# First attention scores interleaved with half tiles of the last second MLP product, in a fused decoder kernel

## The chip, the cores and the metric

One core of a Trainium2 chip runs the whole kernel as one program. Five engines work beside each other, each through its own list of instructions in order, and wait for each other on semaphores: TensorE (PE, matrix products), VectorE (DVE), ScalarE (ACT), GpSimd (POOL) and SyncE (SP), which here only issues DMA transfers. The metric is the device time of one execution in microseconds (us), as the median of several runs. Smaller is better.

## The reference

Four sequences (B = 4) of T = 512 tokens with D = 256 features go through three parts, each followed by a layer norm:

```
x = layernorm(x + recurrent_block(x))      # gated recurrence, then an MLP:
                                           #   x1 + silu(ln(x1) @ w_mlp1.T + b1) @ w_mlp2.T + b2
x = layernorm(x + attention(x, ctx, ctx))  # 16 heads of 16 features, causal softmax
x = layernorm(x + experts(x))              # 48 experts, each takes its top 64 tokens
```

The change lies at the border of the first and the second part: the second MLP product of the last sequence, and the attention scores of the first one.

## The kernel before

**First stage.** Sequences go through the recurrent block one after the other. `expand` makes the 1024 hidden features in eight products, ACT applies silu (`hidden`), and `shrink` makes the second MLP product: for each of TT = 4 token tiles of 128, eight fp32 products of 128x256 summed in PSUM banks 6 and 7 (line 1706). When the whole of it is done PE raises `m2`, DVE adds it to the residual in `X` (`ln_out`, line 1046) and `ln_out_norm` takes statistics (lines 920, 924), waits for 1/sqrt of the variance from POOL (`root`, lines 715 and 717) and normalizes (line 933). For the last sequence, parts of the attention's preparation for sequence 0 are already mixed with `expand`: transposes of its tokens and the key, query and value projections (`early`, `middle`, `late`). Projected keys and queries are split in bf16 pieces, written to DRAM (`key_out`, `query_out`; lines 557 and 561) and read back by head group (`keys_in`, `queries_in`, line 572: six transfers each) into `KTs` and `QTs`. These share SBUF with the MLP weights: the part of groups 0 and 1 may be filled when the first MLP product is done (`m1`), that of groups 2 and 3 only when `m2` is raised.

**Attention.** 16 heads are 4 groups of 4. Each group is four slots j (key tiles of 128). For each group there are 11 PSUM bank fillings of raw scores, over three banks (`scores`: a causal mask product at line 1819, then the scores at line 1823). DVE takes their maxima (`maxima`, line 1133), `negate` splits the negated maxima in bf16 pieces, PE transposes them (`minus_max`, line 1833) and ACT copies them under the queries (line 1506). Then PE makes the scores again, now less the maximum (`shifted`, line 1849), ACT takes the exponential (line 1518), POOL sets what lies above the diagonal to zero (line 797) and PE multiplies with the values (`values`, line 1862). In the slots of one group, the raw scores of the next group are mixed with the shifted ones of this one, so the first group's raw scores stand alone, ahead of all slots. POOL also fills ones rows of `KTs` for each group (line 775, semaphore `ones`) and adds a bias row to the tokens of a sequence (line 790). `TASKS` puts the projections of the next sequence in the slots: (0, 0) holds the transposes of sequence 1 (`query_in`, line 1761), (0, 3) its query projection (line 1782).

The order on each engine is that of the code. PE before runs the whole last `shrink`, waits for `ln3` (DVE has added the product to the residual), makes the eleven fillings for group (0, 0), fills time with five products that nobody reads (`run_idle`, line 1635), then `minus_max` and the slots. POOL waits with the ones rows of groups 2 and 3 for `m2` and then with `root` for the statistics, all ahead of its first slot. SP issues `query_out(0)` behind `keys_in(0, 0)`, which waits for `m1`.

Of the kernel before, what the change touches and what calls it, by code (L numbers as in the profile page):

```python
# [11 lines left out]
ACT = mybir.ActivationFunctionType  # L12
AX = mybir.AxisListType

P = 128
B, T, D = 4, 512, 256
TT = T // P
# [6 lines left out]
MT = MLP // P  # L24
NH, HD = 16, 16
GH = 4
NG = NH // GH
# [104 lines left out]
def build(nc, x, ctx_in, w_in, w_gate, w_out, coupling, w_mlp1, w_mlp2, w_q, w_kv, w_o, w_r,  # L132
# [7 lines left out]
    with stack:  # L140
        def sb(name, shape, dt=F32):
            return stack.enter_context(nc.sbuf_tensor(name, shape, dt))
# [39 lines left out]
        rden = sb("rden", [P, TT, GH])  # L182

# [314 lines left out]
        def _(sp):  # L498
# [98 lines left out]
            tokens_in(1)  # L597
            sp.wait_ge(b2_out, 16 * NPC)
            sp.wait_ge(m1.s, m1.now(B - 1, MT))
            keys_in(0, 0)  # L600
            query_out(0)
# [78 lines left out]
        def _(pool):  # L680
# [91 lines left out]
            for g in range(NG):  # L772
                if g == 2:
                    pool.wait_ge(m2.s, m2.now(B - 1, 1))
                pool.tensor_copy(KTs[SK:SX, GH * g:GH * g + GH, :],
                                 own[SK:SX, :].unsqueeze(2).to_broadcast([SX - SK, GH, T]))\
                    .then_inc(ones, 1)
            pool.wait_ge(ones, NG)
            root(ln3, rs3, B - 1, 1 + 2 * TT)
            pool.wait_ge(rs3.s, rs3.now(B - 1, 2))  # L780
# [12 lines left out]
            def pool_slot(b, g, j, prev, then, *steps):  # L793

                pool.wait_ge(exq.s, exq.now(b, g * NSH + FIRST[j] + len(SHARED[j])))
                pool.sem_inc(pool_held, 1)
                pool.affine_select(out=pb[j % 2][:, :, 0:P], in_=pb[j % 2][:, :, 0:P],  # L797
                                   compare_op=ALU.is_ge, fill=0.0, base=0,
                                   pattern=[[0, GH], [1, P]], channel_multiplier=-1)\
                    .then_inc(msk.s, 1)  # L800
                for name, c, k in steps[0] + steps[1] + steps[2] + steps[3]:
                    if name == "bias":
                        with_bias(c)
                    elif name == "stats":
                        root(ln4, rs4, c, 2 + 2 * TT)
# [99 lines left out]
        def _(dve):  # L905
# [143 lines left out]
            def ln_out_norm(b):  # L1049

                dve.wait_ge(ln3.s, ln3.now(b, 1))
                statistics(ln3, X, b * TT, b, 1)
                norm(ln3, rs3, X, lambda t: X[:, b * TT + t, :], b * TT, b)
# [21 lines left out]
            with dve.Fori(0, B - 2) as b:  # L1075
                recurrence(b + 1)
                ln_out(b)
                ln_out_norm(b)
            recurrence(B - 1, then=False)
            ln_out(B - 2)  # L1080
            ln_out_norm(B - 2)
# [112 lines left out]
            def dve_slot(b, g, j, prev, then, *steps):  # L1194
# [12 lines left out]
                if j == 2 and then is not None:  # L1207
                    negate(*then)
                dve_do(steps[3])
# [3 lines left out]
            ln_out(B - 1)  # L1213
# [5 lines left out]
            ln_out_norm(B - 1)  # L1219
# [185 lines left out]
        def _(act):  # L1405
# [154 lines left out]
            act_do(late)  # L1560
            spare_banks[:] = 5, 7
# [66 lines left out]
        def _(pe):  # L1628
# [61 lines left out]
            def expand(b, tiles):  # L1690

                pe.wait_ge(xe2.s, xe2.now(b, KT))
                for m in tiles:
# [5 lines left out]
                    mm.then_inc(m1.s, 1)  # L1699

# [136 lines left out]
            def shifted(b, g, j):  # L1837

                w = T - j * P
                for n, heads in enumerate(SHARED[j], FIRST[j]):  # L1840
                    if j == 0 and heads[0] % 2 == 0:
                        pe.wait_ge(nte.s, nte.now(b, 2 * g + heads[0] // 2 + 1))
# [108 lines left out]
            shrink(B - 1, range(TT))  # L1951
            for k in range(2):
                pe.wait_ge(*read_by[k])

            pe.wait_ge(silu.s, silu.now(B - 1, MT))
            pe.wait_ge(ln3.s, ln3.now(B - 1, 1))
            read_by.update({0: None, 1: None})
            spare_banks[:] = 5, 7
            for share in SCORED:
                for banks in share:  # L1960
                    scores((0, 0), banks)
            run_idle(5, 4)
            minus_max(0, 0)
            pe.wait_ge(ones, NG)
# [209 lines left out]
```

## Time and profile before

| | |
|---|---|
| time, median of 3 runs | 659.65 us (658.91 to 660.65) |
| time of the profiled execution | 660.65 us |
| its span, first to last instruction | 658.9 us |
| mean granted TensorE clock | 0.964 of full |
| last second MLP product on PE | 166.1 to 180.1 us |
| first shifted scores of group (0, 0) on PE | 191.00 us |
| first shifted scores of group (0, 1) on PE | 206.77 us |

Positions are microseconds from the span's start. The profiled execution's own time is 1.75 us above its span and 1.0 us above the median. In rows of the trace, "x8" after an operation is a count of merged instructions, and what stands in brackets is the idle time of the engine ahead of them and who ended it. One fp32 product is often shown as two instructions.

### The profile page before, as it was taken

What the parts mean: (1) busy time and instruction counts of PE and PEld (TensorE: products, weight loads), DVE (VectorE), ACT (ScalarE), POOL (GpSimd) and SP (SyncE); (2) the same over time, 40 slices, a digit from 0 to 9 for tenths busy, and PEclk for the clock granted to TensorE, in tenths of its full rate; (3) what the DMA queues carried; (4) which work ended last, traced back from release to release, by engine and by line L of the source; (5) the groups of instructions that cost most, each with busy time, mean ns of one, the idle gap of its engine ahead of it and who ended that gap; (6) DMA issues with size and microseconds to landing.
All of it is one profiled execution on the core that took longest, in us unless ns stands there. A gap on an engine that the chain in (4) does not pass through costs nothing.

```text
span 658.9 us, 11028 instructions
## 1 busy us (share of the span) xinstructions
PE 577.2 (88%) x3856; PEld 333.5 (51%) x3856; DVE 380.2 (58%) x792; ACT 275.8 (42%) x460; POOL 186.3 (28%) x231
## 2 busy tenths in 40 slices
PE   6899999999979889989999988850499999999994
PEld 3648586655834535555464444320144554545581
DVE  5874737333176767685697767069633433434645
ACT  4260512425046656666667657500043333333204
POOL 3133232061123123121222222110234444342233
PEclk9999999999989899999999989985699999999998
DMA  8696000013530641155025731049179999999873
GB/s 264 212 381 239 0 0 0 1 67 98 163 94 0 186 119 49 49 178 176 17 91 166 228 157 65 0 154 422 35 270 386 395 395 397 402 392 391 273 268 128
DMA packets 43583, 120.38 MB, mean 183 GB/s; under 512 B 6212, under 2 KB 28308, under 8 KB 40468
## 3 DMA queue, kind: packets, MB, share of 16 engines
q1 hardware_dynamic: 38372, 113.20, 47.5%
q0 software_dynamic: 4320, 6.03, 4.2%
q10 hardware_dynamic: 848, 0.60, 0.3%
q8 instruction: 24, 0.39, 0.2%
q14 instruction: 19, 0.16, 0.1%
HBM read 95.88 MB, written 21.83 MB: 179 GB/s over the span
## 4 chain that ended last, share of the span: by engine, by line
PE 72%; DVE 11%; ACT 7%; DMA 4%; issue 3%; SPq 1%; POOL 1%; ACTq 0%; DVEq 0%; POOLq 0%
PE PS L2026 13%; PE PS L1697 8%; PE PS L1706 8%; PE PS L1782 4%; PE PS L1862 4%; PE PS L1849 4%; PE PS L1823 4%; PE PS L2058 4%; PE PS L2039 4%; DVE Mx L1133 2%; ACT arena L1506 2%; PE PS L1801 2%; PE PS L1666 2%; PE PS L1819 2%; PE PS L1774 2%
## 5 line engine op out<-in xcount | busy, mean ns | idle before, releaser
L1133 DVE TENSOR_REDUCE Mx<-PS 128x1 f32<-128x384 f32 (+3 forms) x176 | 103.6, 634 | 40.0 <-PE PS L1823 38.7
L1518 ACT ACTIVATE arena<-PS 128x512 f32<-128x512 f32 (+1 forms) x176 | 90.3, 559 | 48.1 <-PE PS L1849 46.7
L797 POOL TENSOR_SCALAR_AFFINE_SELECT arena<-arena 128x512 f32<-128x512 f32 x64 | 40.9, 638 | 165.0 <-ACT arena L1518 165.0
L1849 PE MATMUL PS<-arena 108*128 108x512 bf16 (+3 forms) x256 | 62.3, 306 | 11.7 <-ACT arena L1506 5.7
L1823 PE MATMUL PS<-arena 96*128 96x128 bf16 (+3 forms) x256 | 62.8, 303 | 0.0
L1697 PE MATMUL PS<-arena 128*128 128x512 f32 x128 | 56.1, 593 | 3.2 <-ACT arena L1423 1.6
L1706 PE MATMUL PS<-arena 128*128 128x256 f32 x256 | 55.9, 379 | 0.0
L1635 PE MATMUL PS<-ident,identb 128*128 128x512 bf16 x82 | 23.7, 434 | 33.2 <-DVE Y L1258 29.3
L1300 DVE COPY X<-PS 128x512 f32<-128x512 f32 x24 | 16.6, 691 | 61.6 <-PE PS L2026 61.6
L1706 PEld LDWEIGHTS PS<-arena 128*128 128x128 f32 x256 | 48.6, 190 | 6.6
L1590 ACT ACTIVATE X<-X 128x512 f32<-128x512 f32 x48 | 29.4, 630 | 52.7 <-DVE X L1307 52.6
L1862 PE MATMUL PS<-arena 128*32 128x128 f32 (+3 forms) x512 | 47.1, 441 | 1.0 <-POOL arena L797 1.0
L1819 PE MATMUL PS<-causal,identb 128*128 128x128 bf16 (+2 forms) x176 | 44.1, 251 | 4.3 <-DVE X L1046 1.7
L1506 ACT ACTIVATE arena<-PS 12x1024 bf16<-12x1024 bf16 x32 | 30.8, 1009 | 38.8 <-PE PS L1833 38.7
L2026 PE MATMUL PS<-ring_a,X 128*64 128x512 f32 x192 | 43.8, 599 | 0.5 <-ACT X L1579 0.5
L2026 PE MATMUL PS<-arena,X 128*64 128x512 f32 x192 | 43.8, 599 | 0.0
L1849 PEld LDWEIGHTS PS<-arena 108*128 108x128 bf16 x256 | 21.6, 98 | 40.1 <-ACT arena L1518 13.0
L1697 PEld LDWEIGHTS PS<-arena 128*128 128x128 f32 x128 | 24.2, 190 | 32.5 <-issue 31.9
L1307 DVE TENSOR_TENSOR X<-PS,Y 128x512 f32<-128x512 f32 x48 | 31.0, 686 | 10.7 <-PE PS L2039 9.3
L1423 ACT ACTIVATE arena<-PS,vec 128x512 f32<-128x512 f32 x16 | 11.4, 775 | 59.4 <-PE PS L1644 59.4
L855 POOL DMA_INDIRECT sums<-row x14 | 22.3, 1593 | 47.9 <-DVE row L1318 41.9
L715 POOL TENSOR_SCALAR ve<-mv 128x4 f32<-128x4 f32 x16 | 3.7, 229 | 107.2 <-DVE mv L924 98.5
(217 smaller groups left out, 966.5 us busy)
## 6 DMA issues: line engine op xcount, KB each, us to landing
ring_a<-experts SPq DMA_DIRECT2D x12, 2048.0 KB, 15.5
arena<-experts SPq DMA_DIRECT2D x12, 2048.0 KB, 16.5
arena<-pieces SPq DMA_DIRECT2D x192, 64.0 KB, 2.3
ring_a<-experts SPq DMA_DIRECT2D x12, 512.0 KB, 14.9
sums<-zrow SPq DMA_DIRECT2D x3, 2048.0 KB, 20.1
arena<-experts SPq DMA_DIRECT2D x12, 512.0 KB, 16.0
pieces<-arena SPq DMA_DIRECT2D x4, 768.0 KB, 3.9
pieces<-ring_a SPq DMA_DIRECT2D x4, 768.0 KB, 3.7
```

Source lines behind the costliest of these rows:

```text
L797: pool.affine_select(out=pb[j % 2][:, :, 0:P], in_=pb[j % 2][:, :, 0:P], compare_op=ALU.is_ge, fill=0.0, base=0, pattern=[[0, GH], [1, P]] ...
L1133: dve.tensor_reduce(Mx[:, g % 2, i, heads[0]:heads[-1] + 1], bank(score_banks[(g * NSH + u) % 3])[:, 0:len(heads) * w] .rearrange("p (h n) ...
L1307: dve.tensor_tensor(hb[:, a * 512:(a + 1) * 512].rearrange("p (c n) -> p c n", c=8), bank(3 + a).rearrange("p (c n) -> p c n", c=8), b1_s[ ...
L1506: act.activation(QTs[SK:SX, GH * g + 2 * m:GH * g + 2 * m + 2, :], wide(spare(0).bitcast(BF16)[SK:SX, 0:T], 2), ACT.Copy)\
L1518: act.activation(pb[j % 2][:, heads[0]:heads[-1] + 1, 0:w], bank(exp_banks[(g * NSH + n) % 2])[:, 0:len(heads) * w] .rearrange("p (h n) -> ...
L1697: mm = pe.matmul(bank(HIDDEN[m % 4]), wm1_s[:, k, m * P:(m + 1) * P], xT2[:, k, :], start=(k == 0), stop=(k == KT - 1))
L1706: mm = pe.matmul(PS[:, 6 * 512 + t * D:6 * 512 + (t + 1) * D], hid[:, m, t * P:(t + 1) * P], wm2_s[:, m, :], start=(m == 0), stop=(m == MT ...
L1819: pe.matmul(o[:, 0:len(heads) * w].rearrange("p (h n) -> p h n", h=len(heads)) [:, :, i * P:w], identb[:], wide(causal[:], len(heads)), st ...
L1823: mm = pe.matmul(o[:, a * w:(a + 1) * w], QTs[0:SK, g * GH + h, i * P:(i + 1) * P], KTs[0:SK, g * GH + h, 0:w], start=False, stop=True, sk ...
L1849: mm = pe.matmul(bank(exp_banks[(g * NSH + n) % 2])[:, a * w:(a + 1) * w], KTs[0:SX, g * GH + h, j * P:(j + 1) * P], QTs[0:SX, g * GH + h, ...
L1862: mm = pe.matmul(bank(6)[VW * h:VW * (h + 1), j * P:T], Vb[:, j, g * GH + h, :], pb[j % 2][:, h, 0:T - j * P], start=(j == 0), stop=(j == ...
L2026: mm = pe.matmul(bank(1 + n)[CAP * e:CAP * (e + 1), :], xgT[:, k, CAP * e:CAP * (e + 1)], w1_of[u][:, e, k, n * 512:(n + 1) * 512], start= ...
```

## The change

- PE: the last `shrink` is cut into eight halves (four hidden tiles of one token tile each, `shrink_half`). The raw scores of group (0, 0) go between them: three halves, three fillings, a half, three, a half, three, a half, two, a half, `minus_max`, a half. The wait for `ln3` ahead of the scores is gone (the second transposes of the first slot now carry it), as are the five idle products. The wait for `ones` moves to the first shifted product of each group of sequence 0 and asks for that group's rows alone.
- DVE: maxima and `negate` of group (0, 0) come ahead of `ln_out(B - 1)`; statistics follow it, and its normalization moves to the end of the last slot of group (0, 0).
- POOL: ones rows of groups 2 and 3 and `root` move into the first three slots.
- ACT: one exponential of a single column stands ahead of `minus_max`, so the table for the exponential is loaded there.
- SP: `query_out(0)` is issued ahead of `keys_in(0, 0)`.

```diff
+            query_out(0)
             sp.wait_ge(b2_out, 16 * NPC)
             sp.wait_ge(m1.s, m1.now(B - 1, MT))
             keys_in(0, 0)
-            query_out(0)
             queries_in(0, 0)
...
+                if (b, g) == (0, 0):
+                    pool.wait_ge(m2.s, m2.now(B - 1, 1))
+                    if j < 2:
+                        pool.wait_ge(msk.s, msk.now(0, j + 1))
+                        own_rows(2 + j)
+                    elif j == 2:
+                        root(ln3, rs3, B - 1, 1 + 2 * TT)
...
+                if (b, g, j) == (0, 0, TT - 1):
+                    ln_out_norm(B - 1)
                 dve_do(steps[3])
 
             spare_banks[:] = 2, 3
             dve_do(early + middle + late)
-            ln_out(B - 1)
             spare_banks[:] = 5, 7
             for share in SCORED:
                 for banks in share:
                     maxima((0, 0), banks)
             negate(0, 0)
-            ln_out_norm(B - 1)
+            ln_out(B - 1)
+            ln_out_statistics(B - 1)
...
+            act.activation(exp_first[:], ident[:, 0:1], ACT.Exp)
...
+            def shrink_half(b, t, half):
+
+                per = MT // 2
+                for m in range(half * per, (half + 1) * per):
+                    mm = pe.matmul(PS[:, 6 * 512 + t * D:6 * 512 + (t + 1) * D],
+                                   hid[:, m, t * P:(t + 1) * P], wm2_s[:, m, :],
+                                   start=(m == 0), stop=(m == MT - 1))
+                if (t, half) == (TT - 1, 1):
+                    mm.then_inc(m2.s, 1)
...
-            shrink(B - 1, range(TT))
+            pe.wait_ge(silu.s, silu.now(B - 1, MT))
+            first_scores = [n for share in SCORED for banks in share for n in banks]
+            spare_banks[:] = 5, 7
+            for t, half in ((0, 0), (0, 1), (1, 0)):
+                shrink_half(B - 1, t, half)
             for k in range(2):
                 pe.wait_ge(*read_by[k])
-
-            pe.wait_ge(silu.s, silu.now(B - 1, MT))
-            pe.wait_ge(ln3.s, ln3.now(B - 1, 1))
-            read_by.update({0: None, 1: None})
-            spare_banks[:] = 5, 7
-            for share in SCORED:
-                for banks in share:
-                    scores((0, 0), banks)
-            run_idle(5, 4)
+            read_by.update({0: None, 1: (ln3.s, ln3.now(B - 1, 1))})
+            scores((0, 0), first_scores[0:3])
+            shrink_half(B - 1, 1, 1)
+            scores((0, 0), first_scores[3:6])
+            shrink_half(B - 1, 2, 0)
+            scores((0, 0), first_scores[6:9])
+            shrink_half(B - 1, 2, 1)
+            scores((0, 0), first_scores[9:])
+            shrink_half(B - 1, 3, 0)
             minus_max(0, 0)
-            pe.wait_ge(ones, NG)
+            shrink_half(B - 1, 3, 1)
```

On PE, at the end of the first stage, the order before is this (line 1706 is the second MLP product, 1819 and 1823 are mask and scores, in brackets the semaphores that are waited for):

```order
L1706 MATMUL PS<-arena 128x256 [waits silu,ln3]
L1706 MATMUL PS<-arena 128x256 x31
L1819 MATMUL PS<-causal,identb 128x512 [waits ln3,kq_in0,silu,mxs,vev]
L1823 MATMUL PS<-arena 128x128 x4
L1819 MATMUL PS<-causal,identb 128x2x128 [waits mxs]
```

And now, with the lines of the changed kernel (1722 is the second MLP product, 1846 and 1850 are mask and scores):

```order
L1722 MATMUL PS<-arena 128x256 [waits silu,ln3]
L1722 MATMUL PS<-arena 128x256 x11
L1846 MATMUL PS<-causal,identb 128x512 [waits kq_in0,mxs,vev]
L1850 MATMUL PS<-arena 128x128 x4
L1846 MATMUL PS<-causal,identb 128x2x128 [waits mxs]
L1850 MATMUL PS<-arena 128x256 x2
L1846 MATMUL PS<-causal,identb 128x2x128 [waits mxs]
L1850 MATMUL PS<-arena 128x256 x2
L1722 MATMUL PS<-arena 128x256 x4
```

The scores now stand behind 12 of the 32 products instead of behind all of them; their wait for `ln3` is gone and that for the pieces of group 0 (`kq_in0`) is left, with 20 products queued behind it.

On POOL, from the ones rows to the fourth slot, before (775 ones rows, 715 and 717 `root`, 797 the causal select of a slot, 790 the bias row):

```order
L775 CAST arena<-own 12x2048 [waits m1,owns,vset]
L775 CAST arena<-own 12x2048
L775 CAST arena<-own 12x2048 [waits m2]
L775 CAST arena<-own 12x2048
L715 TENSOR_SCALAR ve<-mv 128x4 [waits ones,ln3]
L717 TENSOR_TENSOR rstd<-ve,mhalf 128x4 [waits rs3]
L797 AFFINE_SELECT arena<-arena 128x4x128 [waits rs3,exq]
L797 AFFINE_SELECT arena<-arena 128x4x128 [waits exq] x2
L790 TENSOR_TENSOR X<-X,row 128x1024 [waits xs_in]
```

And now (777 ones rows, 800 the select, 717 and 719 `root`, 793 the bias row):

```order
L777 CAST arena<-own 12x2048 [waits m1,owns,vset]
L777 CAST arena<-own 12x2048 [waits ones]
L800 AFFINE_SELECT arena<-arena 128x4x128 [waits ones,exq]
L777 CAST arena<-own 12x2048 [waits msk,m2]
L800 AFFINE_SELECT arena<-arena 128x4x128 [waits ones,exq]
L777 CAST arena<-own 12x2048 [waits msk,m2]
L800 AFFINE_SELECT arena<-arena 128x4x128 [waits ones,exq]
L717 TENSOR_SCALAR ve<-mv 128x4 [waits m2,ln3]
L719 TENSOR_TENSOR rstd<-ve,mhalf 128x4 [waits rs3]
L793 TENSOR_TENSOR X<-X,row 128x1024 [waits xs_in]
L800 AFFINE_SELECT arena<-arena 128x4x128 [waits exq]
```

Two casts and `root` have moved from ahead of the first select to places between the four selects of the first group, where PE waits for each select.

## Rows read from the trace of the kernel before

**Rows 1.** The page: busy time of the engines, and the chain that ended last by engine.

```profile
PE 577.2 (88%) x3856; PEld 333.5 (51%) x3856; DVE 380.2 (58%) x792; ACT 275.8 (42%) x460; POOL 186.3 (28%) x231
PE 72%; DVE 11%; ACT 7%; DMA 4%; issue 3%; SPq 1%; POOL 1%; ACTq 0%; DVEq 0%; POOLq 0%
```

**Rows 2.** Chain that ended last, in order of time: start us, us, what.

```profile
180.23 1.24 DVE X L1046
...
191.82 1.28 ACT L1518
```

**Rows 3.** Timeline of PE: start us, us, line, operation, count, idle ahead and its releaser.

```profile
166.14 13.98 PE L1706 MATMUL PS<-arena 128*128 128x256 f32 x64
181.82 0.38 PE L1819 MATMUL PS<-causal,identb 128*128 128x512 bf16 x1 [1.69 <-DVE X L1046]
...
187.21 1.24 PE L1635 MATMUL PS<-ident,identb 128*128 128x512 bf16 x5
...
191.00 0.59 PE L1849 MATMUL PS<-arena 108*128 108x512 bf16 x2 [1.15 <-issue]
...
199.36 0.22 PE L1819 MATMUL PS<-causal,identb 128*128 128x128 bf16 x1
...
199.63 0.22 PE L1819 MATMUL PS<-causal,identb 128*128 128x128 bf16 x1
...
201.29 3.65 PE L1782 MATMUL PS<-arena,wq_s 128*128 128x512 f32 x8
...
206.77 0.61 PE L1849 MATMUL PS<-arena 108*128 108x512 bf16 x2 [0.69 <-ACT arena L1506]
```

**Rows 4.** Timeline of DVE at the border.

```profile
142.83 2.41 DVE L933 TENSOR_SCALAR X<-X,mv,rstd 128x256 f32<-128x256 f32 x4 [1.58 <-POOL rstd L717]
...
182.52 6.13 DVE L1133 TENSOR_REDUCE Mx<-PS 128x4 f32<-128x512 f32 x11 [1.07 <-PE PS L1823]
...
189.33 1.41 DVE L920 BATCH_NORM_STATS2 stats<-X 128x6 f32<-128x256 f32 x4
...
192.83 1.38 DVE L933 TENSOR_SCALAR X<-X,mv,rstd 128x256 f32<-128x256 f32 x4 [1.56 <-POOL rstd L717]
194.13 0.68 DVE L1133 TENSOR_REDUCE Mx<-PS 128x4 f32<-128x512 f32 x1
...
202.00 1.37 DVE L1143 TENSOR_SCALAR nst<-Mx 128x16 bf16<-128x16 f32 x1
```

**Rows 5.** Timeline of POOL at the border.

```profile
180.19 3.73 POOL L775 CAST arena<-own 12x2048 bf16<-12x2048 f32 x2 [13.44 <-PE PS L1706]
191.45 0.23 POOL L715 TENSOR_SCALAR ve<-mv 128x4 f32<-128x4 f32 x1 [7.53 <-DVE mv L924]
...
196.33 0.65 POOL L797 TENSOR_SCALAR_AFFINE_SELECT arena<-arena 128x512 f32<-128x512 f32 x1 [3.54 <-ACT arena L1518]
...
200.97 2.35 POOL L790 TENSOR_TENSOR X<-X,row 128x1024 f32<-128x1024 f32 x1
```

**Rows 6.** Timeline of SP's DMA issues, then DMA issues of that stretch with us to landing.

```profile
163.38 3.42 SPq L572 DMA_DIRECT2D arena<-pieces  x6
166.84 0.42 SPq L561 DMA_DIRECT2D pieces<-ring_a  x1
170.69 20.40 SPq L572 DMA_DIRECT2D arena<-pieces  x42
...
arena<-pieces SPq DMA_DIRECT2D x48, 64.0 KB, 2.3
pieces<-arena SPq DMA_DIRECT2D x1, 768.0 KB, 4.5
pieces<-ring_a SPq DMA_DIRECT2D x1, 768.0 KB, 3.8
```

**Rows 7.** Windows: length, busy PE, PEld, DVE, ACT, POOL, then granted clock, DMA.

```profile
181.50:191.00 9.50, 6.10 (x37) 2.43 (x38) 8.23 (x21) 1.12 (x2) 2.42 (x2) 1.00 0.52 142
191.00:207.00 16.00, 15.05 (x97) 7.50 (x98) 11.66 (x25) 11.26 (x19) 6.08 (x7) 0.89 0.04 11
```

More of the change, by code:

```diff
@@ L182, in build @@
         rden = sb("rden", [P, TT, GH])
+        exp_first = sb("exp_first", [P, 1])
         used = [0]
@@ L771, in _, with own_rows @@
             pool.wait_ge(m1.s, m1.now(B - 1, MT))
-            for g in range(NG):
-                if g == 2:
-                    pool.wait_ge(m2.s, m2.now(B - 1, 1))
+            def own_rows(g):
                 pool.tensor_copy(KTs[SK:SX, GH * g:GH * g + GH, :],
@@ L777, in _ @@
                     .then_inc(ones, 1)
-            pool.wait_ge(ones, NG)
-            root(ln3, rs3, B - 1, 1 + 2 * TT)
-            pool.wait_ge(rs3.s, rs3.now(B - 1, 2))
+                pool.wait_ge(ones, g + 1)
+            for g in range(2):
+                own_rows(g)
             for g in (xob, msk, rs4):
@@ L1047, in ln_out, with ln_out_statistics, ln_out_norm @@
                                   ALU.add).then_inc(ln3.s, 1)
-            def ln_out_norm(b):
+            def ln_out_statistics(b):
                 dve.wait_ge(ln3.s, ln3.now(b, 1))
                 statistics(ln3, X, b * TT, b, 1)
+            def ln_out_norm(b):
                 norm(ln3, rs3, X, lambda t: X[:, b * TT + t, :], b * TT, b)
@@ L1077, in _ @@
                 ln_out(b)
+                ln_out_statistics(b)
                 ln_out_norm(b)
@@ L1080, in _ @@
             ln_out(B - 2)
+            ln_out_statistics(B - 2)
             ln_out_norm(B - 2)
@@ L1840, in shifted @@
                 for n, heads in enumerate(SHARED[j], FIRST[j]):
+                    if (b, j, heads[0]) == (0, 0, 0):
+                        pe.wait_ge(ones, g + 1)
                     if j == 0 and heads[0] % 2 == 0:
```

## The prediction

> **What bounds the kernel now.** I read the page first: PE is busy 88% of the span and makes up 72% of the chain that ended last [rows 1]. A change at the border pays if it takes out time in which PE does nothing useful, and if nothing later swallows it. So I followed the chain through the border [rows 2] and laid the timelines of PE, DVE, POOL and SP beside it [rows 3 to 6].
>
> The last second MLP product runs on PE without a gap from 166.14 to 180.1. The first shifted scores start at 191.00 [rows 3]. In the 10.9 us between, PE has only the eleven score fillings, one small transpose and five idle products (1.24 us). The rest is a string of handovers, none of which needs the product: DVE adds the product to the residual (1.24 us, rows 2; PE idle 1.69 us, rows 3), the fillings then go at the pace of DVE's eleven maxima (6.13 us from 182.52, rows 4), negation follows up to 189.33, then transpose and ACT's copy. Behind 191.00 the chain goes over ACT's table load, 1.28 us from 191.82 [rows 2], and PE's granted clock is 0.89 in the mean from 191 to 207, against 1.00 from 181.5 to 191 [rows 7]. With two levels, 2.4 GHz (1.00) and 1.2 GHz (0.50), that is 0.11 x 16 / 0.5 = 3.5 us at the lower one. Ahead of it PE was busy for 6.10 of 9.50 us.
>
> **The change, part by part.** I count from 166.14, the start of the product, which nothing in the change moves, to the first shifted scores of group (0, 1), which stood at 206.77 [rows 3]. Behind that point both orders are alike but for one normalization on DVE.
>
> *First part: 166.14 to the first shifted scores.* Before 191.00 - 166.14 = 24.86 us. After, PE needs:
> - the product, 13.98 us, unchanged in amount; half a token tile is 13.98 / 8 = 1.75 us [rows 3];
> - eleven fillings. Where nothing holds them, mask and scores start 199.63 - 199.36 = 0.27 us apart [rows 3], so 11 x 0.27 = 3.0, and some 0.2 more for the first, which has four small score products: 3.2 us. The three or two maxima between two blocks of fillings take 3 x 0.56 = 1.7 us (6.13 / 11, rows 4), about one half's 1.75, so DVE's pace is hidden behind halves of the product;
> - the transpose of the negated maxima, 0.4. DVE ends the last two maxima and the negation (189.33 - 188.65 = 0.7) some 2.1 us after the last filling; the half behind it covers 1.75 of this: 0.3 of waiting;
> - a wait for the pieces of group 0. The scores come up at 166.14 + 3 x 1.75 = 171.4. Before, `query_out` was issued at 166.84, and the queries' six transfers could start at 170.69; they go out every 20.40 / 42 = 0.49 us and land 2.3 us after issue [rows 6], so group 0 was complete at 170.69 + 2.4 + 2.3 = 175.4. After, `query_out` leaves as soon as its pieces exist, at about 163.3 (just before 163.38, when SP began the keys, rows 6). The queue is then fuller, so I take the 4.5 us of the other write rather than 3.8 [rows 6] and 0.4 for its issue: queries start at 168.2 and are complete at 172.8. PE waits 1.4 us. The bounds: 0, if they land by 171.4, and 4.0, if nothing is won over 175.4.
>
> Sum 13.98 + 3.2 + 0.4 + 0.3 + 1.4 = 19.3 us: the first shifted scores start at 185.4, 5.6 us earlier. The five idle products are in the time saved.
>
> *Second part: to the first shifted scores of group (0, 1).* Before 206.77 - 191.00 = 15.77 us. Three chains run here.
> - DVE now does the residual add and the statistics where it before did statistics, wait and normalization. After `m2` at 185.4 it adds (1.24, rows 2) and takes statistics, 1.9 us (189.33 until POOL's root was released at 191.45, less a hop), so the maxima of group (0, 1) start at 188.65 against 194.13 [rows 4, 5]. PE ends slot 1 when four of them are done and one filling: 188.65 + 0.7 x 3 + 0.5 + 0.3 = 191.5. Before, that point was 197.6, with PE at half clock on the way and the table load ahead of it. This is 6.1 us earlier, half a us more than the first part: DVE, not PE, sets it now, so I don't count the clock and the table load (together over 2 us) in full.
> - From there PE's work is the same up to the query projection at 201.29 and ACT's copy behind it, which released 206.77 [rows 3], 9.1 us: the group starts at 200.65.
> - POOL now has four selects of 0.65, two casts of 1.87 (3.73 / 2), root (191.45 to 192.83, 1.4) and the bias row of 2.35 in a row [rows 4, 5]: 2.6 + 3.7 + 1.4 + 2.35 = 10.1 us, with hops 10.4. The first select came 5.33 us after the first shifted scores (196.33 - 191.00); without the table load 4.05, so at 189.45. POOL ends at 199.85. PE needs the last select to finish the values just ahead of 200.65: hidden, with 0.8 us to spare. If that cover were gone (each op 10% longer), a us would be lost.
>
> The normalization (1.38 us, rows 4) now stands at the end of DVE's slot 3, behind the projections' remainders at about 200.4, and ends at 201.8. The first maximum of group (0, 2) is wanted at about 201.9: just hidden. The second transposes now wait for the residual add at 186.7, when PE gets there at 186.9. SP's pieces for groups 2 and 3 wait for `m2` as before, now 5.3 us later, and go out in 24 x 0.49 = 11.8 us; the last lands near 199.5, and group 3 is needed after 210, group 2 after 201 with half of that time. The single exponential runs in ACT's idle time ahead of 185.
>
> On a row of DVE there is something against the change: the same four normalizing instructions took 2.41 us at 142.83, beside small POOL work, and 1.38 us at 192.83, and one tiny negation took 1.37 us at 202.00, while POOL had its bias row from 200.97 [rows 4, 5]. POOL work is what the change puts among DVE's. The casts, though, took 1.87 us each beside DVE's add and maxima, no longer than expected. So I leave the sum as it is and hold 1.0 us for the range. The Trainium skill (SBUF — State Buffer, the section on its two sides) says that the port pair which DVE and GpSimd share is an exclusive lock, and that the loser blocks for the whole instruction. By that rule a normalizing instruction can block for a whole select or bias row, and the sum would be up to 2.35 us more. The trace agrees in one place: the long negation ended at 203.37 and the bias row at 203.32.
>
> The table load's row is 1.28 us, and the exponential starts right behind it, at 193.1. The Trainium skill (ScalarE: Activation LUTs, What ACT_TABLE_LOAD costs) counts a drain of 1.38 us beside the load of 1.28. By it the move would be worth 2.66 us of ACT's time; no drain shows here between the copies and the load, and the sum takes neither.
>
> Total 206.77 - 200.7 = 6.1 us; I take 6.0. Against the profiled execution's own 660.65 that is 654.65. Its own time is 1.0 above the median, so the forecast of a median is 659.65 - 6.0 = 653.65, rounded to 653.7.
>
> Does it stay? Behind this point every engine waits for others, not for something with a time of its own. The weights of the experts are loaded behind semaphores of the attention's end, so they move along.
>
> **Rivals.**
> - *Pieces late.* The write of the query pieces queues behind the tokens and context that SP issues just ahead of it, and lands little earlier. PE waits up to 4.0 us instead of 1.4, with 20 products behind the wait. For it: the write of the keys, in such company, took 4.5 us, not 3.8 [rows 6]. Against: to lose all of it the write would have to take 7.3 us. Price up to 2.6 us: 655 to 656.3. Chance 0.15.
> - *POOL or DVE gives some back in the first group.* The 0.8 us of cover is used up, and the port costs 1 to 2 us: about 655.5. Chance 0.10.
> - *More than counted.* A later low-clock stretch falls away too, or the gain of clock and table counts in full: 651.5. Chance 0.10.
> - *Nothing gained.* The border's shift is absorbed by a later wait with a time of its own, or the fillings are paced as slowly as before. I see no such wait. 659.65, chance 0.06.
> - *Slower: the clock.* The new wait for the pieces sits in the middle of a product that now runs at full clock without a gap. If it makes the granted clock fall to its lower level, and PE stays there for the rest of the product, the remaining 20 of 32 products take 8.7 us more (13.98 x 20 / 32), and 653.65 + 8.7 = 662.4. It decides from 6 us of loss, about 14 products at half clock. Against it: before, PE idled 1.69 us ahead of 181.82 and the clock stayed at 1.00 up to 191 [rows 3, 7], and the low stretch behind that lasted some 3.5 us. Such a fall costs 1.8: still faster. Chance of slower by this 0.04.
> - The likeliest case, 5 to 7 us gained, has 0.55.
>
> **Numbers.** What a measurement of this kernel can tell from no change is about 0.3%, 2.0 us: faster is below 657.7. All cases but the last two named are there: 0.55 + 0.15 + 0.10 + 0.10 = 0.90, less 0.02 for the tail of late pieces with a clock fall. The range takes in the late pieces and the port on one side (656.9) and the uncounted clock on the other (651.0).
>
> **What would show it.** In the changed kernel's profile: the first score filling starts at 172.8 with an idle time of 1.4 us before it, released by DMA; the last product ends near 185.4; the table load lies at about 163.5; the first shifted scores start at 185.4 and those of group (0, 1) at 200.7; POOL's fourth select ends before 200; the clock is 1.00 through 200. It is wrong if the fillings start after 175, if the clock falls between 172 and 186, or if the span shrinks less than that second mark moves.

## The result and the profile after

The changed kernel takes 657.26 us, the median of 11 runs (653.99 to 660.39), against 660.9 us for the kernel before, measured beside it (11 runs, 658.91 to 664.44): a ratio of 0.9944, 95% interval 0.9922 to 0.9965. It is faster by 0.56%, 3.6 us between the medians, where 6.0 were forecast; the time lies 0.4 us above the forecast's range. A second set of 12 runs gave 657.32 us and 0.9943 (0.9918 to 0.9969). The profiled execution of the first set is one of its longest, 660.11 us, span 658.3. Two single runs among the experiments below, 1348 us in e0 and 872 us in e10, were slow ones and are left out of the ratios but not of the table's medians, which without them are 661.30 and 652.45 us.

PE's timeline of the changed kernel at the border:

```profile
166.14 5.35 PE L1722 MATMUL PS<-arena 128*128 128x256 f32 x24
174.07 0.38 PE L1846 MATMUL PS<-causal,identb 128*128 128x512 bf16 x1 [2.59 <-DMA arena<-pieces]
...
175.18 3.55 PE L1722 MATMUL PS<-arena 128*128 128x256 f32 x8
...
179.26 1.89 PE L1722 MATMUL PS<-arena 128*128 128x256 f32 x8
...
186.37 2.00 PE L1722 MATMUL PS<-arena 128*128 128x256 f32 x8
188.20 0.60 PE L1878 MATMUL PS<-arena 108*128 108x512 bf16 x2
...
202.84 0.43 PE L1891 MATMUL PS<-arena 128*32 128x128 f32 x8 [0.38 <-POOL arena L800]
203.57 0.59 PE L1878 MATMUL PS<-arena 108*128 108x512 bf16 x2 [0.30 <-issue]
```

Against [rows 3], the first shifted scores (line 1878, before 1849) moved from 191.00 to 188.20 and those of group (0, 1) from 206.77 to 203.57: 3.2 us won. Two things differ from the working. The wait for the pieces of group 0 is 2.59 us, not 1.4. And the half product behind it took 3.55 us where the next one took 1.89. The windows show why (columns as in rows 7, the granted clock is the third number from the end):

```profile
175.00:176.00 1.00, 1.00 (x7) 0.80 (x5) 1.00 (x3) 0.00 (x0) 0.00 (x0) 0.62 0.52 152
176.00:177.00 1.00, 1.00 (x4) 0.81 (x3) 0.67 (x2) 0.00 (x0) 0.00 (x0) 0.50 0.49 135
178.00:179.00 1.00, 1.00 (x6) 0.53 (x6) 0.00 (x0) 0.00 (x0) 0.00 (x0) 0.68 0.26 74
179.00:180.00 1.00, 1.00 (x8) 0.88 (x6) 0.99 (x3) 0.00 (x0) 0.00 (x0) 1.00 0.00 0
```

Just behind the wait the clock went to its lower level, 1.2 GHz, and back before 179. The DMA issues of the changed kernel from 160 to 176 us answer to [rows 6]:

```profile
pieces<-ring_a SPq DMA_DIRECT2D x1, 768.0 KB, 6.1
Y<-X SPq DMA_DIRECT2D x1, 512.0 KB, 6.1
```

The write of the query pieces landed 6.1 us after its issue, which was 3.8 us before the change. The transfers of context and tokens, 512 KB each, were issued ahead of it, at 159.26 and 159.84, and the tokens took 6.1 us themselves; before, the write went out at 166.84, when both had landed. DVE and POOL, to compare with [rows 4, 5]:

```profile
203.13 1.37 DVE L943 TENSOR_SCALAR X<-X,mv,rstd 128x256 f32<-128x256 f32 x4
204.71 0.69 DVE L1147 TENSOR_REDUCE Mx<-PS 128x4 f32<-128x512 f32 x1 [0.21 <-PE PS L1850]
```

```profile
192.19 0.64 POOL L800 TENSOR_SCALAR_AFFINE_SELECT arena<-arena 128x512 f32<-128x512 f32 x1 [25.33 <-ACT arena L1534]
...
199.84 2.36 POOL L793 TENSOR_TENSOR X<-X,row 128x1024 f32<-128x1024 f32 x1
202.14 0.65 POOL L800 TENSOR_SCALAR_AFFINE_SELECT arena<-arena 128x512 f32<-128x512 f32 x1
```

The normalization is hidden: DVE then still waits 0.21 us for PE. POOL's string of four selects, two casts, root and bias takes 202.79 - 192.19 = 10.6 us, and PE waited 0.38 us for its end.

### The profile page after: what moved, and what is told of

It is laid out like the page before. It is cut to its first block, busy times and chain, and to the rows that moved or that the text cites. A ratio compares the mean times of both kernels' runs of the same rounds, so it can differ in the third digit from the quotient of the medians.

```text
span 658.3 us, 11020 instructions
## 1 busy us (share of the span) xinstructions
PE 578.8 (88%) x3851; PEld 334.5 (51%) x3851; DVE 379.3 (58%) x792; ACT 276.4 (42%) x461; POOL 186.4 (28%) x231
## 4 chain that ended last, share of the span: by engine, by line
PE 51%; DVE 10%; ACT 5%; issue 2%; POOL 1%; DMA 0%; DVEq 0%; ACTq 0%; POOLq 0%
PE PS L2059 13%; PE PS L1891 4%; PE PS L1878 4%; PE PS L2091 4%; PE PS L1850 4%; PE PS L2072 4%; PE PS L1809 3%; PE PS L2101 2%; PE PS L1828 2%; PE PS L1846 2%; DVE Mx L1147 2%; ACT arena L1522 2%; PE PS L1801 2%; DVE Y L1275 2%; DVE Y L1274 2%
## 5 line engine op out<-in xcount | busy, mean ns | idle before, releaser
L1733 PE MATMUL PS<-arena 128*128 128x256 f32 x192 | 41.9, 379 | 0.0
L1714 PEld LDWEIGHTS PS<-arena 128*128 128x128 f32 x128 | 24.2, 190 | 32.4 <-issue 31.8
L1733 PEld LDWEIGHTS PS<-arena 128*128 128x128 f32 x192 | 36.6, 190 | 4.9
L1850 PEld LDWEIGHTS PS<-arena 96*128 96x128 bf16 x256 | 24.6, 101 | 14.8 <-issue 2.3
```

The source lines that it names most:

```text
L1714: mm = pe.matmul(bank(HIDDEN[m % 4]), wm1_s[:, k, m * P:(m + 1) * P], xT2[:, k, :], start=(k == 0), stop=(k == KT - 1))
L1733: mm = pe.matmul(PS[:, 6 * 512 + t * D:6 * 512 + (t + 1) * D], hid[:, m, t * P:(t + 1) * P], wm2_s[:, m, :], start=(m == 0), stop=(m == MT ...
L1850: mm = pe.matmul(o[:, a * w:(a + 1) * w], QTs[0:SK, g * GH + h, i * P:(i + 1) * P], KTs[0:SK, g * GH + h, 0:w], start=False, stop=True, sk ...
```

## Experiments

Every kernel was timed beside the kernel before on the same chip; e3_again and e8 to e10 were timed on another chip than the rest, so between the two groups the ratios are what compares. Times in the table are medians of 6 to 12 runs, ratios are against the kernel before with their 95% intervals; "first" and "second mark" are the starts on PE of the first shifted scores and of those of group (0, 1), each in the one profiled execution.

| label | what | us | ratio | first | second mark |
|---|---|---|---|---|---|
| e0_before_again | before, once more | 661.35 | 0.9961 to 1.0016 | 190.84 | 206.61 |
| e6_table_alone | before, table load moved | 660.33 | 0.995 to 1.0007 | 191.00 | 206.60 |
| (the change) | | 657.26 | 0.9922 to 0.9965 | 188.20 | 203.57 |
| e1_again | the change, once more | 657.32 | 0.9918 to 0.9969 | 186.54 | 201.91 |
| e5_query_late | write back behind the keys | 659.72 | 0.9945 to 0.9992 | 191.04 | 206.41 |
| e2_idle_fill | idle products in the wait | 657.46 | 0.9893 to 0.9953 | 186.61 | 201.97 |
| e4_four_halves | four halves first | 656.44 | 0.9902 to 0.9958 | 187.55 | 203.03 |
| e7_ones_later | ones rows one group later | 657.94 | 0.9923 to 0.9969 | 186.53 | 202.69 |
| e9_fill_second | idle products before (0, 2) | 657.95 | 0.9901 to 0.9959 | 186.47 | 201.84 |
| e3_queue_clear | tokens, context after pieces | 653.46 | 0.985 to 0.9916 | 185.71 | 201.07 |
| e3_again | the same | 654.28 | 0.9852 to 0.9922 | 185.72 | 201.09 |
| e8_combined | e3 and a new order of halves | 653.26 | 0.9835 to 0.9906 | 184.96 | 200.33 |
| e10_combined_fill | e8 and e9 | 652.78 | 0.9824 to 0.9897 | 185.03 | 200.40 |

### The change once more

> The changed kernel once more, for a second profile. Theory A (the wait for the pieces in the middle of the product makes the granted clock fall): the first score filling again comes near 174.0 us after a wait of 2.6 us, the clock falls to the lower level within 1.5 us of it, the first shifted scores stand at 188.2 and those of group (0,1) at 203.6; time near 657.3 us. Rival B (the clock falls by a phase of its own, not by the wait): the low stretch lies elsewhere in this execution, and the first shifted scores come at 186.5. Rival C (what is missing is lost behind the border, by low stretches that differ between executions): the marks at the border repeat, and the time differs from the first profile's by more than 1 us.

The same kernel, with the same wait, but this time the clock held. PE's timeline of e1_again and its window over the product:

```profile
174.09 0.38 PE L1846 MATMUL PS<-causal,identb 128*128 128x512 bf16 x1 [2.60 <-DMA arena<-pieces]
...
175.20 1.89 PE L1722 MATMUL PS<-arena 128*128 128x256 f32 x8
...
201.91 0.59 PE L1878 MATMUL PS<-arena 108*128 108x512 bf16 x2 [0.30 <-issue]
```

```profile
174.00:180.00 6.00, 5.91 (x39) 4.82 (x40) 3.63 (x7) 0.00 (x0) 0.00 (x0) 1.00 0.38 111
```

The second mark is 1.66 us earlier than in the first profile, 4.86 us earlier than before the change. So the wait of 2.6 us repeats to 0.01 us, and the low stretch (of the clock at its lower level) does not: three more profiles with the same wait (this one, e7, e9) are without it. Theory A in its strict form is refuted: the wait doesn't make the clock fall each time.

### The kernel before once more

> The kernel before once more, for a second profile. If low stretches of the clock fall differently in each execution, the one at 192 to 196 us may be missing here; then group (0,1) starts at 205.8 instead of 206.77 and the marks behind it keep that distance except where another low stretch comes or goes (1.5 us each). If they belong to the schedule, the profile repeats within 0.3 us.

Here the low stretch at 192 to 196 came back, and the mark at 206.61 repeats within 0.16 us. It is there in all three profiles with the old order (before, this one, e6); in none of the profiles with the new order does a low stretch lie between 190 and 210. The one near 222 to 226 is in them too; behind 380 us they differ. The window of e0_before_again:

```profile
191.00:207.00 16.00, 15.21 (x97) 7.57 (x96) 11.51 (x23) 11.34 (x19) 6.08 (x7) 0.89 0.04 9
```

### Idle products in the wait

```diff
                 shrink_half(B - 1, t, half)
+            run_idle(11, 4)
             for k in range(2):
                 pe.wait_ge(*read_by[k])
```

> Eleven idle products (2.4 us) stand in PE's wait for the pieces, so the scores start as late as before (174.1) but PE isn't idle. Theory A: the clock stays at 1.00 through the product, group (0,1) starts 1.65 us earlier (201.9), time near 655.6 us. Rival B: the low stretch stays, 203.6 and 657.3 us. Rival C: the mark moves, the median by less than half of it.

PE's idle time fell to 0.31 us, the clock held in the profile, and the mark was 201.97. The median is that of the changed kernel, 657.46 against 657.32. A low stretch that comes in one profile of four can't cost the median its full 1.65 us, and filling the wait won nothing that can be measured.

### The write of the query pieces back behind the keys

```diff
-            query_out(0)
             sp.wait_ge(b2_out, 16 * NPC)
             sp.wait_ge(m1.s, m1.now(B - 1, MT))
             keys_in(0, 0)
+            query_out(0)
             queries_in(0, 0)
```

> The changed kernel with the write of the query pieces back behind the reads of the keys. Pieces of group 0 then land near 175.4 us, PE waits 4.0 instead of 2.6 us, and group (0,1) starts 1.4 us later than in a profile of the changed kernel without a low stretch in the product (203.3). Time near 658.7 us if a longer wait brings no more low clock, near 660 us if it makes the clock fall each time.

The scores start at 175.82, after 4.38 us of waiting; in this execution the clock fell while PE was still waiting, and was at its lower level for most of 174 to 182:

```profile
175.82 0.58 PE L1846 MATMUL PS<-causal,identb 128*128 128x512 bf16 x1 [4.38 <-DMA arena<-pieces]
...
177.91 3.62 PE L1722 MATMUL PS<-arena 128*128 128x256 f32 x8
...
191.04 0.60 PE L1878 MATMUL PS<-arena 108*128 108x512 bf16 x2
```

```profile
174.00:182.00 8.00, 6.17 (x25) 4.52 (x26) 2.05 (x4) 0.00 (x0) 0.00 (x0) 0.57 0.40 114
```

The second mark is 4.5 us later than in e1_again: 1.73 us for the landing (175.82 - 174.09), the rest for the clock. The median rose by 2.4 us (659.72 against 657.32, with 661.5 for the kernel before beside either). Of a gain of some 4.2 us, 1.8 us are left (ratio 0.9969): more than half of the change's gain hangs on SP's one moved line.

### The queue cleared ahead of the write

```diff
-            context_in(1)
-            tokens_in(1)
             query_out(0)
             sp.wait_ge(b2_out, 16 * NPC)
             sp.wait_ge(m1.s, m1.now(B - 1, MT))
             keys_in(0, 0)
             queries_in(0, 0)
+            tokens_in(1)
+            context_in(1)
```

> SP issues the write of the query pieces ahead of the context and the tokens of sequence 1 and these only behind the reads of group 0. Theory A, with the queue as the reason of the late pieces: the write lands in 3.8 to 4.5 us instead of 6.1, the pieces of group 0 are there at 172.1 instead of 174.0, the wait is 0.7 us and too short for the clock to fall; group (0,1) at 200.0 to 200.3, time near 653.9 us. If the queue isn't the reason: landing stays at 6.1 us and nothing moves (657.3). Rival B: only the wait is won, 655.4 us.

> The cleared queue once more, for a second profile and more times. Its first median was 3.9 us under that of the changed kernel, though its mark at the border was only 0.84 us earlier. If the rest is fewer low stretches that the cleared queue brings with it, this profile again has none between 186 and 370 us and the median is again near 653.5. If it was luck of that call: low stretches as in the changed kernel, median near 656 us.

DMA issues and PE's timeline of e3_queue_clear:

```profile
pieces<-ring_a SPq DMA_DIRECT2D x1, 768.0 KB, 5.4
Y<-X SPq DMA_DIRECT2D x1, 512.0 KB, 3.3
```

```profile
173.26 0.38 PE L1846 MATMUL PS<-causal,identb 128*128 128x512 bf16 x1 [1.84 <-DMA arena<-pieces]
...
201.07 0.59 PE L1878 MATMUL PS<-arena 108*128 108x512 bf16 x2 [0.31 <-issue]
```

The write takes 5.4 us instead of 6.1, and the mark comes 0.84 us earlier: half of what was expected. What was issued ahead of the write is part of the reason; the reads of the keys, which are issued right behind it, may be the other part (before, nothing was issued behind it until it had landed); that was not tried. That company behind a write can matter shows on the write of the keys, issued at 158.8 in both kernels. In the changed kernel, with context and tokens behind it, it takes 4.5 us. In e3_queue_clear, with nothing behind it, it takes 3.8:

```profile
pieces<-arena SPq DMA_DIRECT2D x1, 768.0 KB, 3.8
```

The times fell more than the mark, by 3 to 4 us in both sets. Some of it is clock: in the first profile nothing is low between 186 and 370 us, in the second the stretch at 216 to 222 is there again. The windows of e3_queue_clear and of e3_again:

```profile
216.00:222.00 6.00, 5.50 (x50) 4.16 (x42) 3.42 (x9) 4.76 (x8) 0.61 (x1) 1.00 0.76 235
```

```profile
216.00:222.00 6.00, 5.50 (x38) 4.23 (x30) 1.88 (x5) 3.61 (x6) 0.00 (x0) 0.72 0.76 231
```

### Four halves ahead of the scores

```diff
-            for t, half in ((0, 0), (0, 1), (1, 0)):
+            for t, half in ((0, 0), (0, 1), (1, 0), (1, 1)):
...
             scores((0, 0), first_scores[0:3])
-            shrink_half(B - 1, 1, 1)
+            shrink_half(B - 1, 2, 0)
             scores((0, 0), first_scores[3:6])
-            shrink_half(B - 1, 2, 0)
+            shrink_half(B - 1, 2, 1)
             scores((0, 0), first_scores[6:9])
-            shrink_half(B - 1, 2, 1)
+            shrink_half(B - 1, 3, 0)
             scores((0, 0), first_scores[9:])
-            shrink_half(B - 1, 3, 0)
             minus_max(0, 0)
             shrink_half(B - 1, 3, 1)
```

> Four halves of the product instead of three stand ahead of the first scores, and none between the last scores and the transposes of the maxima. The wait for the pieces shrinks from 2.6 to 0.9 us, but DVE's last maxima and negation (2.1 us) are now uncovered. Theory A: no fall of the clock, the two other terms cancel, group (0,1) at 201.9, time near 655.6 us. Rival B: fall as before, 203.6 and 657.3 us.

The wait for the pieces went to 0.92 us and the transposes waited 1.85 us for DVE, as the working had them. The transposes stood at 184.43, as in e1_again (184.39), and then the clock fell, here at 185 where the first profile of the change had it at 175:

```profile
184.43 0.39 PE L1860 MATMUL PS<-identb,nst 128*12 128x128 bf16 x4 [1.85 <-DVE nst L1164]
...
187.55 1.06 PE L1878 MATMUL PS<-arena 108*128 108x512 bf16 x2
```

The median, 656.44, is within noise of the changed kernel. Moving the gap from one place of the product to another won nothing that can be measured.

### The table load alone

```diff
+        ve_first = sb("exp_first", [P, 1])
...
+            act.activation(ve_first[:], ident[:, 0:1], ACT.Exp)
             spare_banks[:] = 5, 7
             minus_max(0, 0)
```

> The kernel before with one change: the single exponential ahead of the transposes of the maxima, so the table load leaves the border. If DVE's chain (statistics, wait for the root, normalization) sets the pace behind the first shifted scores, as the prediction says, group (0,1) moves by 0.5 us or less and the time stays within noise of before. If the 1.28 us of the load are on the path in full: 1.3 us off. If a drain came with it as the skill's page has it: 2.7 us off.

ACT's timeline of e6_table_alone:

```profile
189.88 1.93 ACT L1507 ACTIVATE arena<-PS 12x1024 bf16<-12x1024 bf16 x2 [24.91 <-PE PS L1835]
191.83 1.09 ACT L1519 ACTIVATE arena<-PS 128x512 f32<-128x512 f32 x2
```

The first exponential starts at 191.83 instead of 193.12, 1.29 us earlier: the load's own length, with no drain beside it. The second mark moved by 0.17 us only (206.60), because DVE's chain was the longer one: its normalization stood at 192.82, against 192.83 before, and its maxima behind it. 0.9979 (0.995 to 1.0007) is no change that can be told.

### Ones rows one group later

```diff
-                if (b, g) == (0, 0):
-                    pool.wait_ge(m2.s, m2.now(B - 1, 1))
-                    if j < 2:
-                        pool.wait_ge(msk.s, msk.now(0, j + 1))
-                        own_rows(2 + j)
-                    elif j == 2:
-                        root(ln3, rs3, B - 1, 1 + 2 * TT)
+                if (b, g, j) == (0, 0, 2):
+                    pool.wait_ge(m2.s, m2.now(B - 1, 1))
+                    root(ln3, rs3, B - 1, 1 + 2 * TT)
+                if (b, g) == (0, 1) and j < 2:
+                    pool.wait_ge(msk.s, msk.now(0, TT + j + 1))
+                    own_rows(2 + j)
```

> The changed kernel with the ones rows of groups 2 and 3 in the slots of group (0,1) instead of (0,0): 3.8 us less on POOL between the first four selects. If POOL's chain is only level with PE's, as the profile after has it (PE waited 0.38 us for the last select), group (0,1) moves by 0 to 0.3 us and the time by no more than that (657.0). If POOL set the pace of the first slots, group (0,1) comes 1 us or more earlier (656.2).

Neither: the mark came 0.78 us later (202.69 against 201.91). DVE's and POOL's timeline of e7_ones_later, then DVE's of e1_again:

```profile
197.39 2.38 DVE L1160 SCALAR_TENSOR_TENSOR nst<-Mx,nst 128x16 bf16<-128x16 f32 x1
```

```profile
197.38 2.34 POOL L793 TENSOR_TENSOR X<-X,row 128x1024 f32<-128x1024 f32 x1
```

```profile
197.40 0.18 DVE L1161 SCALAR_TENSOR_TENSOR nst<-Mx,nst 128x16 bf16<-128x16 f32 x1
```

With POOL ahead of its old schedule, the bias row began 0.01 us ahead of a negation on 16 elements with both inputs in SBUF, and that took 2.38 us instead of 0.18, until the bias row was done. PE then waited 1.12 us for what DVE does behind it:

```profile
201.15 0.22 PE L1859 MATMUL PS<-identb,nst 128*12 128x128 bf16 x1 [1.12 <-DVE ring_a L1110]
```

In the changed kernel the two casts happen to hold the bias row back until the negation is over. The rule that the prediction took from the Trainium skill (SBUF — State Buffer, the section on its two sides), that whoever comes second to the shared port pair blocks for the whole instruction, is borne out here, and it costs 0.8 us on the path.

### Idle products ahead of group (0, 2)

```diff
-                pe.wait_ge(mneg.s, mneg.now(b, 4 * (g + 1)))
-                o = take(0, nte, nte.now(b, 2 * g + 2)).bitcast(BF16)
+                if (b, g) == (0, 2):
+                    o = take(0, nte, nte.now(b, 2 * g + 2)).bitcast(BF16)
+                    run_idle(6, 5)
+                    pe.wait_ge(mneg.s, mneg.now(b, 4 * (g + 1)))
+                else:
+                    pe.wait_ge(mneg.s, mneg.now(b, 4 * (g + 1)))
+                    o = take(0, nte, nte.now(b, 2 * g + 2)).bitcast(BF16)
```

> The changed kernel with six idle products in PE's wait of 1.6 us for the negated maxima of group (0,2), the place ahead of the low stretch at 216 to 222 us. If PE's idle time there makes the clock fall, the stretch is gone, ACT's copies of group (0,3) come 14.0 us behind those of (0,2) instead of 15.5, and the time falls by up to 1.5 us (655.8). If the idle time doesn't matter: stretch and time as in the changed kernel, 657.3.

In the profile the stretch is gone. The windows of e1_again and of e9_fill_second:

```profile
216.00:222.00 6.00, 5.36 (x44) 4.15 (x45) 2.01 (x3) 3.67 (x6) 0.05 (x1) 0.72 0.64 203
```

```profile
216.00:222.00 6.00, 5.42 (x56) 4.31 (x57) 3.31 (x8) 4.75 (x8) 0.00 (x0) 1.00 0.65 203
```

ACT's copies of group (0, 3) come 14.03 us behind those of (0, 2), against 15.52 in e1_again: 1.5 us is the price of one low stretch. But the median is 657.95, not lower. As the stretch was also missing in e3's first profile and in those of e4 and e7, without idle products, one profile doesn't show that they did it.

### The combined versions

```diff
             scores((0, 0), first_scores[3:6])
-            shrink_half(B - 1, 2, 0)
-            scores((0, 0), first_scores[6:9])
             shrink_half(B - 1, 2, 1)
-            scores((0, 0), first_scores[9:])
+            scores((0, 0), first_scores[6:])
             shrink_half(B - 1, 3, 0)
```

This stands on e3's order on SP, with (1, 1) ahead of the scores and (2, 0) between the first two blocks.

> Cleared queue, four halves ahead of the scores, and the last five fillings in one block, so that a half of the product stands again between the last scores and the transposes. The wait for the pieces falls to 0.1 us, and 0.9 us are given back in waits for maxima: first shifted scores near 184.8, group (0,1) near 200.2 against 201.07 with the cleared queue alone. Time 0.9 us under that of the cleared queue of this call if the border is on the path, the same if POOL's chain (10.6 us of selects, casts, root and bias) holds the group back.

> The combined version with the six idle products as well. If both act by themselves it is the fastest, 651 to 652.5 us. If the cleared queue's schedule has no low stretch there anyway, the idle products change nothing against the combined version.

PE's timeline of e8_combined:

```profile
173.41 0.38 PE L1846 MATMUL PS<-causal,identb 128*128 128x512 bf16 x1 [0.17 <-issue]
...
182.81 0.39 PE L1860 MATMUL PS<-identb,nst 128*12 128x128 bf16 x4 [0.36 <-DVE nst L1164]
...
200.33 0.59 PE L1878 MATMUL PS<-arena 108*128 108x512 bf16 x2 [0.30 <-issue]
```

Both marks are within 0.2 us of the forecast. 653.26 us (e8) is 1.0 us under e3_again, which was measured beside it, and the 652.45 us of e10 are 1.8 us under it; their intervals overlap its own, but lie below that of the changed kernel. The ratio of e10 is 0.986 (0.9824 to 0.9897). Against e8 it shows nothing of the idle products: e8's profile has no low stretch there without them.

## Why the prediction was off

**The mechanism held.** The removal of the handovers pays, and all terms of the sum but the wait for the pieces came out: in e1_again the path from the product's start to the first shifted scores is 20.4 us, of it 2.60 for the pieces, so 17.8 for all the rest, where the working has 17.9. From there to group (0, 1) the working gave 15.3 us; both profiles of the changed kernel have 15.37. The table load lies in idle time (163.48), and the wait at the transposes is about 0.3 us. POOL was at the end of its cover, not 0.8 us inside it: its last select ends at 201.12 in e1_again, not before 200, and PE waited 0.38 us for it. ACT's copy hid this but for little: from the start of ACT's copies for group (0, 1) to its first shifted scores it is 1.12 us, and 1.07 before.

**The step that failed first: the wait for the pieces, "0.4 for its issue" and 4.5 us to land.** The write went out at 163.19, as forecast, but landed after 6.1 us, 1.6 more than the term says. The 0.4 for the issue took back a part: the trace counts the landing from the start of the issue, so 4.5 had it in. The queries started at 169.4 instead of 168.2, the rest of this term held, and PE waited 2.6 us instead of 1.4. The mark without any low stretch is 201.91 where 200.7 was forecast: this term alone. It was the rival "pieces late" at half its price. That the term hangs on the queue's order is shown from both sides: 1.73 us later with the write behind the keys, 0.84 us earlier with the queue cleared.

**The step that failed second: "the clock is 1.00 through 200".** In the first profile a low stretch lay over the product, 175 to 179, and cost 1.65 us: 1.2 and 1.65 make up the 2.9 us that the second mark fell short there. The stretch isn't bound to the wait; it was in one of four profiles with it. The rival "the clock" named the place and had too high a price for it (8.7 us); it put a fall of some 3.5 us at 1.8 us, which is near.

**The base: "its own time is 1.0 above the median".** The forecast took this 1.0 off the profiled execution, to 653.65 us. The median of 659.65 was that of three runs. Eleven runs gave 660.9 us, and three later sets of 14 to 34 runs 661.5 to 661.9. So of the 3.6 us between 653.65 and 657.26, 1.25 us are the base and 2.4 us the gain. Without this the time would lie inside the range; the gain would still be 3.6 us and not 6.0.

**What the sum left out: the clock behind the border.** The first profile is 3.2 us ahead at group (0, 1), yet its span is 0.6 us shorter. That was one of the prediction's own signs of being wrong, as was the fall of the clock between 172 and 186. I followed ACT's copies for each group. The lead is 3.2 us up to the last group of sequence 1, 3.7 to 382 us, and 1.85 us from 396 on. The windows of before, then those of the changed kernel's first profile:

```profile
380.00:388.00 8.00, 5.39 (x43) 3.47 (x44) 3.56 (x7) 5.18 (x9) 1.87 (x2) 0.79 0.63 266
408.00:416.00 8.00, 6.09 (x46) 2.96 (x44) 2.37 (x8) 6.61 (x11) 0.80 (x2) 1.00 0.24 94
```

```profile
380.00:388.00 8.00, 7.29 (x32) 4.59 (x31) 3.87 (x7) 5.16 (x10) 0.63 (x1) 0.57 0.17 68
408.00:416.00 8.00, 6.53 (x34) 2.17 (x34) 0.77 (x3) 5.47 (x10) 0.05 (x1) 0.79 0.01 2
```

The change's execution had 6.9 us at the lower level where before had 3.4, and another 3.4 us behind 408, where before had none. Low stretches that cost some 1.5 us each come and go, in every kernel. Among the changed kernel's 11 runs the fastest (653.99 us) had a mean clock of 0.970 and the slowest (660.39) one of 0.959. With (1 - clock) x span / 0.5 that is 39 and 54 us at the lower level: 15 us more of low clock, 6.4 us more of time. The kernel before spreads by 5.5 us in 11 runs. A single profile of either can't carry a sum to 1 us, which mine did.

**"Does it stay?" was right.** Two executions with alike low stretches behind the border show it, e0_before_again and e1_again. These are ACT's copies for group (0, 1) and for the last group of sequence 3, first of the kernel before, then of the change:

```profile
205.54 1.93 ACT L1506 ACTIVATE arena<-PS 12x1024 bf16<-12x1024 bf16 x2
...
411.57 1.93 ACT L1506 ACTIVATE arena<-PS 12x1024 bf16<-12x1024 bf16 x2 [0.36 <-PE PS L1833]
```

```profile
200.79 1.92 ACT L1522 ACTIVATE arena<-PS 12x1024 bf16<-12x1024 bf16 x2
...
406.75 1.92 ACT L1522 ACTIVATE arena<-PS 12x1024 bf16<-12x1024 bf16 x2 [0.36 <-PE PS L1860]
```

The lead is 4.75 us at the first and 4.82 at the second, and the spans are 659.7 and 654.9 us: what the border won arrives in full at the end. In the first pair of profiles low clock ate it, and no wait with a time of its own shows.

**What stays open.** The mark without a low stretch is 4.86 us earlier, the medians 3.6 and 4.2 us. The difference fits a low stretch in the product now and then (one profile in four, at 1.65 us, makes 0.4 us), but was not counted over the runs. Why the cleared queue's times fell by 3 to 4 us for 0.84 us of mark is open too: its 12 runs had less low clock than the changed kernel's 23 (44 us in the mean against 47). A us of low clock costs at most half a us, so this makes at most 1.6 us; some 1 us has no cause shown. And what decides on a low stretch is not settled: PE's idle time ahead of it is the same in executions with and without it (2.6 us ahead of 175, 1.6 us ahead of the stretch near 216).

## What to carry to other kernels

When work is pulled forward, the chain that it waited on becomes the new wait: here scores were free of the residual but then stood on a DRAM round trip, and without one moved line in the DMA queue the gain was 1.8 us instead of 4.2. Time a transfer in the company that it will have, not alone. A removed table load is worth what the longest chain beside it leaves over, which was 0.17 of 1.28 us here. Where the spread of the runs comes from the clock, take marks from profiles for the mechanism and medians of many runs for the size, of the kernel before too.

## What the runs showed of the hardware

The same program with the same waits had low stretches of the granted clock in different places in different executions, 1.5 to 1.65 us lost at each; filling 2.6 us of PE's idle time with products moved no median. A DVE instruction on 16 elements lasted 2.38 us because a POOL instruction had begun 0.01 us ahead of it. And a DRAM write of 768 KB took 3.8, 5.4 or 6.1 us to land, by what was issued around it.
